# Relational graph layer: the first tile of each quad multiplied over the whole 510-column window, and one count matmul for four tiles

## What is computed

```
def _rgcn_layer(x, src, dst, edge_type, w_rel, root, bias):
    seg = dst * NUM_REL + edge_type
    sums = segment_sum(x[src], seg, N * NUM_REL)
    cnt = segment_sum(ones, seg, N * NUM_REL)
    mean = (sums / maximum(cnt, 1.0)[:, None]).reshape(N, NUM_REL, -1)
    return einsum('nrd,rdo->no', mean, w_rel) + x @ root + bias
edge_type = argmax(edge_attr[:, 16:26], axis=1)
h = relu(_rgcn_layer(x, ...)); y = _rgcn_layer(h, ...)
return layernorm(x + y)
```

## Time and profile before

| | |
|---|---|
| median of 3 runs | 4824.44 us (4823.83 to 4830.43) |
| the profiled execution's own time | 4821.75 us |
| its span | 4819.8 us |
| busy share | PE 50%, weight loads 44%, DVE 44%, ACT 20%, POOL 62% |
| mean granted clock of TensorE | 0.684 of 2.4 GHz |
| gathers | 3126 of 128 rows, 205.07 MB |

### The profile page before, as it was taken

How to read it: one execution, slowest core, us unless ns; L and a number is a source line. 1 busy time by engine, 2 the same in 40 slices (tenths; PEclk the granted TensorE clock), 3 DMA queues, 4 the chain that set the end, 5 groups by cost and what they waited for, 6 DMA issues and landing times.

```text
span 4819.8 us, 58181 instructions
## 1 busy us (share of the span) xinstructions
PE 2410.4 (50%) x13845; PEld 2126.7 (44%) x13846; DVE 2126.7 (44%) x3980; ACT 979.0 (20%) x3133; POOL 2969.1 (62%) x3140
## 2 busy tenths in 40 slices
PE   2555555555555556555633545434444454444445
PEld 2444445445454455545533434333334443343444
DVE  5444545444444445444533434433343343343435
ACT  0222212112222222222211222212221222221223
POOL 6666666666666666666546666666666666666663
PEclk6676767666666667667766667766766666676667
DMA  4222222222222222222111211212221121212111
GB/s 101 65 59 63 64 62 62 62 63 63 59 65 64 59 63 63 63 62 63 44 35 51 54 52 52 53 51 54 53 53 53 51 54 53 53 53 54 52 53 36
DMA packets 206632, 275.68 MB, mean 57 GB/s; under 512 B 62732, under 2 KB 156428, under 8 KB 206444
## 3 DMA queue, kind: packets, MB, share of 16 engines
q0 software_dynamic: 100032, 205.07, 16.4%
q1 hardware_dynamic: 101534, 67.96, 5.0%
q10 hardware_dynamic: 4878, 0.86, 0.2%
HBM read 260.85 MB, written 12.80 MB: 57 GB/s over the span
## 4 chain that ended last, share of the span: by engine, by line
another core or an unknown queue 37%; issue 22%; DVE 18%; PE 17%; DVEq 5%; ACT 1%; DMA 0%; SPq 0%; ACTq 0%
PE ps_agg L1599 10%; DVE z_s L1899 5%; DVE ring L1856 4%; DVE S L1830 3%; PE ps_agg L1595 3%; DVEq L1834 2%; PE ps_y L1625 2%; PE ps_cnt L1584 1%; DVEq L1855 1%; ACT prod L1504 1%; DVE hit L1821 1%; DVE cnt_ring L1847 1%; DVE amax L1793 1%; DVEq L1856 1%
## 5 line engine op out<-in xcount | busy, mean ns | idle before, releaser
L1306 POOL DMA_INDIRECT rows<-table,idx_s x1563 | 1475.0, 944 | 902.3 <-issue 573.9
L1306 POOL DMA_INDIRECT rows<-in_x_dram,idx_s x1507 | 1431.3, 950 | 875.3 <-issue 463.1
L1856 DVE TENSOR_TENSOR ring<-ps_agg,ring 128x510 f32 x784 | 539.7, 688 | 2231.7 <-remote 1805.5
L1599 PE MATMUL ps_agg<-S,rows 128*128 128x140 f32 x6272 | 1297.1, 363 | 219.7 <-issue 217.5
L1599 PEld LDWEIGHTS ps_agg<-S,rows 128*128 128x128 f32 x6272 | 1248.8, 264 | 289.5 <-issue 241.3
L1595 PE MATMUL ps_agg<-zero_b 128*128 128x510 bf16 x784 | 402.4, 513 | 1056.4 <-DVE ring L1856 715.9
L1625 PE MATMUL ps_y<-wall,ring 128*128 128x128 f32 x3920 | 646.6, 309 | 549.4 <-issue 546.3
L1625 PEld LDWEIGHTS ps_y<-wall,ring 128*128 128x128 f32 x3920 | 579.4, 221 | 569.2 <-issue 566.2
L1504 ACT ACTIVATE prod<-ps_y,rc_s 128x128 f32<-128x128 f32 x1960 | 542.5, 381 | 1228.8 <-remote 814.2
L1595 PEld LDWEIGHTS ps_agg<-zero_b 128*128 128x128 bf16 x784 | 87.8, 112 | 1162.5 <-DVE ring L1856 665.2
L1899 DVE TENSOR_REDUCE z_s<-prod 128x128 f32<-128x1536 f32 (+1 forms) x196 | 564.9, 2882 | 15.4 <-ACT prod L1507 14.6
(11 more groups left out here) (111 smaller groups left out, 1050.6 us busy)
## 6 DMA issues: line engine op xcount, KB each, us to landing
attr<-in_edge_attr_dram SPq DMA_DIRECT2D x97, 336.0 KB
rows<-table,idx_s POOLq DMA_INDIRECT x1563
rows<-in_x_dram,idx_s POOLq DMA_INDIRECT x1507
x_in<-in_x_dram SPq DMA_DIRECT2D x97, 64.0 KB
table<-h_s SPq DMA_DIRECT2D x97, 64.0 KB
x_in<-table SPq DMA_DIRECT2D x97, 64.0 KB
prod<-in_x_dram SPq DMA_DIRECT2D x97, 64.0 KB
out_dram<-o_s SPq DMA_DIRECT2D x97, 64.0 KB
```

Source lines behind the costliest of these rows:

```text
L1306: pool.indirect_dma_start(out=rows[:, slot, j, :], out_offset=None, in_=(x, htab)[l][:, :], in_offset=bass.IndirectOffsetOnAxis(ap=at, axi ...
L1599: ins = t_.matmul(ps_agg[h][:, bass.ds(off[j] * R, TCOL)], lhsT=rows[:, o % PER, j, :], rhs=S[:, o % 2, j, :], start=False, stop=(c == 3))
L1856: v_.tensor_tensor(win, ps_agg[h][:, 0:QCOL].rearrange("p (n r) -> p r n", r=R), win, ALU.add).then_inc(agg_taken, 1)
```

## The change

The matmul of zeros in `aggregate` goes. The first tile of each quad gets a one-hot matrix over all 510 columns, and its matmul opens the bank; the other three stay at 140 columns and their offsets. `make_S` becomes three instructions: one for the two first tiles (2 by 510 columns), and one for each half's other three tiles (420 columns). In `count` one bf16 matmul for each half multiplies the type matrices of four tiles, 32 columns each, with their four node matrices, 56 columns; the four wanted pieces of 10 by 14 stand in four partition groups. `add_counts` adds each piece, at its offset, to a ring that now has four partition groups: eight instructions for an octet in place of two, with eight offsets loaded into VectorE's registers (`tile_places`). `turn_counts` adds the four groups with a matmul by a matrix of four stacked identities, `fourth`.

```
 def count(g, sl):
     for h in range(2):
-        t_.matmul(ps_cnt[:, h * 64:h * 64 + QWIN], lhsT=zero_b[:, 0:P], rhs=zero_b[:, 0:QWIN],
-                  start=True, stop=False)
-        for c in range(4):
-            j = 4 * h + c
-            ins = t_.matmul(ps_cnt[:, bass.ds(off[j] + h * 64, TWIN)],
-                            lhsT=hit_typ[:, sl, j * R:j * R + P], rhs=hit[:, sl, j, :],
-                            start=False, stop=(c == 3))
+        ins = t_.matmul(ps_cnt[:, h * 64:h * 64 + 4 * TWIN],
+                        lhsT=hit_typ[:, sl, 4 * h:4 * h + 4, :].rearrange("p c r -> p (c r)"),
+                        rhs=hit[:, sl, 4 * h:4 * h + 4, :].rearrange("p c w -> p (c w)"),
+                        start=True, stop=True)
 def aggregate(l, i, o, off, last):
-        t_.matmul(ps_agg[h][:, 0:QCOL], lhsT=zero_b[:, 0:P], rhs=zero_b[:, 0:QCOL],
-                  start=True, stop=False)
-        for c in range(4):
-            j = 4 * h + c
+        t_.matmul(ps_agg[h][:, 0:QCOL], lhsT=rows[:, o % PER, 4 * h, :],
+                  rhs=S[:, o % 2, h * SQ:h * SQ + QCOL], start=True, stop=False)
+        for c in range(1, 4):
+            j, at = 4 * h + c, h * SQ + QCOL + (c - 1) * TCOL
             ins = t_.matmul(ps_agg[h][:, bass.ds(off[j] * R, TCOL)], lhsT=rows[:, o % PER, j, :],
-                            rhs=S[:, o % 2, j, :], start=False, stop=(c == 3))
+                            rhs=S[:, o % 2, at:at + TCOL], start=False, stop=(c == 3))
 def turn_counts(b, k, octs):
-    t_.transpose(ps_misc[:, 300:300 + R], cnt_ring[:, k * P:(k + 1) * P], ident[0:R, 0:R])
+    t_.matmul(ps_misc[:, 300:300 + R], lhsT=cnt_ring[:, k * P:(k + 1) * P], rhs=fourth[:, :],
+              start=True, stop=True)
 def make_S(l, g, sl):
-    v_.tensor_tensor(S[:, sl, :, :], bc1(ps_iota[:, 0:TCOL], GT, TCOL),
-                     bc(comb_t[:, bass.ds(g * GT, GT)], GT, TCOL), ALU.is_equal)
+    v_.tensor_tensor(hot[:, :, 0:QCOL], bc1(ps_iota[:, 0:QCOL], 2, QCOL),
+                     comb[:, :, 0:1].to_broadcast([P, 2, QCOL]), ALU.is_equal)
+    for h in range(2):
+        ins = v_.tensor_tensor(hot[:, h, QCOL:SQ].rearrange("p (c w) -> p c w", w=TCOL),
+                               bc1(ps_iota[:, 0:TCOL], 3, TCOL), bc(comb[:, h, 1:4], 3, TCOL),
+                               ALU.is_equal)
 def add_counts(g, pos, off):
     for h in range(2):
-        v_.tensor_tensor(win, ps_cnt[0:R, h * 64:h * 64 + QWIN], win, ALU.add)
+        for c in range(4):
+            win = cnt_ring[32 * c:32 * c + R, bass.ds(pos[h] + off[4 * h + c], TWIN)]
+            at = h * 64 + c * TWIN
+            ins = v_.tensor_tensor(win, ps_cnt[32 * c:32 * c + R, at:at + TWIN], win, ALU.add)
```

More of the change, by code:

```diff
@@ L1087 @@
 QCOL = QWIN * R
+SQ = QCOL + 3 * TCOL
 RN = PER * P
@@ L1226, in gnn_kernel @@
         rows = sb("rows", [P, PER, GT, C])
-        S = sb("S", [P, 2, GT, TCOL])
+        S = sb("S", [P, 2, 2 * SQ])
         hit = sb("hit", [P, 2, GT, TWIN], BF16)
-        hit_typ = sb("hit_typ", [P, 2, GT * R + P], BF16)
+        hit_typ = sb("hit_typ", [P, 2, GT, 32], BF16)
         ring = sb("ring", [P, R, RING])
-        cnt_ring = sb("cnt_ring", [R, RING])
+        cnt_ring = sb("cnt_ring", [P, RING])
+        fourth = sb("fourth", [P, R])
         rc_s = sb("rc_s", [P, R])
@@ L1574, in offsets, with count @@
                     return off
-                def count(g, sl, off):
+                def count(g, sl):
                     pe.wait_ge(hit_ready, g + 1)
@@ L1655, in _ @@
                                 if l == 0:
-                                    count(i * (2 * PER) + o, o % 2, off)
+                                    count(i * (2 * PER) + o, o % 2)
                                 aggregate(l, i, o, off, last)
@@ L1766, in _ @@
             link(v_.tensor_copy(pick[:, :], p16[:, 8:16]))
+            link(v_.tensor_copy(fourth[:, :], ident[:, 0:R]))
+            for c in range(1, 4):
+                link(v_.tensor_tensor(fourth[:, :], fourth[:, :], ident[:, 32 * c:32 * c + R], ALU.add))
             link(v_.tensor_tensor(p16[:, 8:16], p16[:, 8:16], p16[:, 0:8], ALU.mult))
@@ L1770, in _ @@
                                   ALU.mult))
-            link(v_.tensor_copy(ps_iota[:, 0:TCOL], iota_c[:, :]))
+            for m in range(0, QCOL, TCOL):
+                n = min(TCOL, QCOL - m)
+                link(v_.tensor_scalar(ps_iota[:, m:m + n], iota_c[:, 0:n], float(m), None, ALU.add))
             fast = dve.value_load(flag_i[0:1, 0:1], min_val=0, max_val=1)
@@ L1837, in places, with tile_places, add_counts @@
                     return pos
-                def add_counts(g, pos):
+                def tile_places(g):
+                    _, off = nc.values_load_multi_w_load_instructions(
+                        off_i[0:1, bass.ds(g * GT, GT)], engines=(DVE_,), min_val=0, max_val=OFFMAX,
+                        skip_runtime_bounds_check_because=IN_RANGE)
+                    return off
+                def add_counts(g, pos, off):
                     for h in range(2):
-                        win = cnt_ring[:, bass.ds(pos[h], QWIN)]
                         if h == 0:
@@ L1952, in _ @@
                                 if l == 0:
-                                    add_counts(g, pos)
+                                    add_counts(g, pos, tile_places(g))
                                 if h == 0:
```

16 lines of the change are left out of this document (8 added, 8 removed).

## The result

| | before | after |
|---|---|---|
| median | 4824.31 us (4823.83 to 4830.43, 5 runs) | 4844.32 us (4839.71 to 4855.13, 5 runs) |
| the profiled execution, its span | 4821.75, 4819.8 us | 4839.71, 4837.7 us |
| mean granted clock | 0.684 | 0.726 |

The ratio is 1.0044 [1.0033, 1.0056]: the changed kernel is slower, by 20 us, where I forecast 86 us. The sign is right, the size is a quarter.

A forecast was written before the change was run, and what follows sets the result against it. POOL's gathers set a floor, with late index copies adding some 395 us; +17 us in the first layer and +69 in the second gave +86, so 4911 us, 1.8% slower, own range 4850 to 4990, whole range 4775 to 5100.

The forecast's parts named there:

- late copies: ScalarE's copies of indices that keep POOL's gathers waiting; about 235 and 160 us in the two layers.
- The floor of 4425 us: POOL's gathers and landing waits if no index copy were ever late: 4820 − 395 us.
- TensorE's and VectorE's terms: Per half +0.85 us on TensorE; per octet counts −0.95 us there, S +0.87 and counts +0.8 us on VectorE, costed at nothing.
- What lies on the path: TensorE's work before late index copies: +0.35 us per four octets in the first layer, +1.4 us in the second.
- the crawl: Late in a long run of gathers, TensorE does one aggregation half at about 0.7 us an instruction, once in four octets.
- my +17: First layer: +0.35 us for each four octets before late copies, 49 times, +17 us.
- +69 us forecast: Second layer: two longer halves before one late copy in four octets, +1.4 us, 49 times.
- The start, the turn between the layers and the end: nothing: Stretches outside the layers' laps, taken as led by transfers and other work; no cost.
- rival A: VectorE becomes the bound, its sums late behind S and counts; 5158 us whole, 5034 with half; chance 0.15.
- C: In the laps, the end of the gathers' run sets the path and hides the extra; 4824 us; chance 0.06.
- D: TensorE's slow stretch goes by columns, not instructions; 360 us at most, about half taken, 5090 us; chance 0.12.
- B: TensorE's wide tile is cheap or hidden and fewer instructions win; 4681 us, about 4800 in milder form; chance 0.17.

The follow-up runs named there:

- e16: The kernel before, unaltered, run for its trace on a chip of the faster sort; 4423.22 us, ratio 1.0000.
- e7: The kernel before with the wide first tile alone, counts as before; 4840.34 us against 4820.58 us, ratio 1.0038.
- e6: The kernel before with the count part of the change alone, matmul of zeros kept; 4809.74 us against 4820.58 us, ratio 0.9975.
- e5: The changed kernel, unaltered, run again beside the kernel before; 4834.65 us against 4820.58 us, ratio 1.0039.
- e9: The kernel before with eight more matmuls of zeros over 14 columns opening each half; 5027.11 us against 4886.02 us, ratio 1.0293.
- e10: The kernel before with the 510-column matmul of zeros made three times in each half; 4930.85 us against 4886.02 us, ratio 1.0099.
- e12: The kernel before with POOL waiting for its rows after every octet, not every second; 4907.22 us against 4886.0 us, ratio 1.0052.
- e8: The kernel before with POOL, after an odd octet, waiting for the previous octet's landing instead of its own; 5065.69 us, ratio 1.0514.

## Why the prediction was wrong

**What bounds it.** Right: gathers, their landing, and late copies. The floor of 4425 us fits 4422 on a chip B, but only in the sum. Of the 399 us between the spans of the kernel before on the two sorts (4819.8 and e16's 4421.1), the two layers' gathers make 199.5 and 139.0, which I had at 235 and 160; the turn makes 39.4 and the end 20.7, which I had not counted.

**TensorE's and VectorE's terms.** Right at the clock 0.50: half 3.10 us, counts 0.25 us; S +1.07 and counts +0.95 on VectorE, a little above. But I priced every half at that clock, and in stretches at 1.00 the wide tile adds 0.49 us and not 0.85. The rule that I weighed, that matmuls start N / 1.2 GHz apart when cold (the Trainium skill, TensorE: Matmul & The Clock Gate, section "Wait — 56ns, not 53.3ns?"), would have made the wide fp32 pair 0.85 us in all. The trace has 1.70, 0.85 for each of the two records, where the rule has 0.43. So it does not hold here for fp32: each record takes twice what the rule gives, as the rows of 140 columns had said.

**What lies on the path: this step failed.** I wrote that from the end of the crawl to the first late copy TensorE does one half, and two halves in the second layer. No such half is on the path: where the copy is late, the second half's signal comes 22.9 us after the run's start in all four kernels with and without the two parts, whatever the halves take, often together with the first's. The slow stretch itself was read rightly, 0.7 us for each instruction late in a run (0.70 in the traces), though the rows with the prediction, matmuls 2.1 us apart, did not show that price by themselves. What was wrong is what ends it. That the records are entries into a queue, as I took it, no run shows. In the first layer my +17 was the sum of two large terms. The wide tile had (0.85 + 1.70 − 0.3) x 49 = +110 us, and e7 shows +5.1 up to the first layer's last gather. The counts had 2 x −0.95 x 49 = −93 us, and e6 shows −11.1. They were some twenty and eight times too large, and they cancelled; that the first layer comes near (+17 forecast, +2.1 and −1.9 seen) is luck. In the second layer nothing cancelled: +69 us forecast, and +8.9, +1.5 and +6.9 us seen in after, e5 and e7.

**"The start, the turn between the layers and the end: nothing".** Wrong. They have 7.0 of the 17.9 us, and 11.9 in e5. After a layer's last gather six or seven octets wait, and no gather hides them. VectorE sets the pace at the end, which is rival A with its mechanism right, in 2% of the span.

**The rivals.** C, "the path is set by the end of the gathers' run and the extra is inside it", is nearest to what the laps do. I gave it 0.06. In the earlier trace rows the two sums before the copy are 3.63 us apart and in the earlier trace rows 2.26, with halves of one length: that the gap was no half's length stood in the rows. D, a crawl by columns, does not fit e9 against e10: few columns cost three times as much as many. B rests on fewer instructions winning; e6 and e9 bear that out in direction, at some 11 us for what I had at over 90. The median, 4844, lies inside the whole range but under the forecast's own range of 4850 to 4990.

**Best version.** The kernel with the new counts and without the wide tile (e6) is 11 us faster than the kernel before and 25 us faster than the changed one on a chip A, and equal to both on a chip B.

## What to carry to other kernels

When the profile shows a slow stretch and then a consumer that starts, compare the times of two consumers that need different amounts of the producer's work: if they start together, the signal and not the work was late, and a longer or shorter producer changes little. Cost the drains (what is left to do after a layer's last transfer) by themselves: the whole buffer ring is left, and there the engine with the longest list pays in full. A difference made of two large terms of opposite sign needs its parts run apart before it is believed.

## What the runs showed of the hardware that I had not expected

The same kernel takes 4422 us on some chips and 4821 to 4886 on others, with gathers spaced alike (944 to 951 ns busy each, all kernels). The difference is the late copies and the longer turn and end. On the slower ones two things go together late in a run of gathers. Instructions take 0.70 us each: register operations of VectorE, elsewhere 0.04 to 0.07 us, and by its distances TensorE's. And signals of TensorE come late, often two together, about 3 us after the run's last gather has ended (the late copies of the first layer before stand 3.16 us behind it in the median, of 42). Pausing the gathers after eight takes most of both away (e12), letting them run on makes it slower (e8). POOL's own wait for the landing of a run's last rows is 2.55 us, half a us shorter, so whether writing the gathers or moving their rows holds the engines is not told apart; no run changed one without the other. Whether the late signals are only the effect of the slow instructions, and what differs between the two sorts of chip, no run here shows either.
